# Integers in place of rounded floats: the feed-forward quantisations of a four-stage transformer kernel, one core

## The chip, the core and the metric

The kernel runs on one core of a Trainium2 chip. The metric is the device time of one launch in microseconds. The core has TensorE (PE, matrix products), VectorE (DVE), ScalarE (ACT), GpSimd (POOL) and SyncE (SP, which issues the transfers). Each has its own instruction stream; they meet only at semaphores.

## The reference, cut to what matters

`x` is 2x256 tokens of width 512. The reference adds four branches to it in turn: a quantised product with the context, a quantised gated feed-forward layer (`_L0_ffn_ref`), cross attention, and a mixture of experts. The change lies in the second:

```
def act_qdq(x, bits=16):
    qmax = 2 ** bits - 1
    mn = minimum(min(x), 0);  mx = maximum(max(x), 0)
    scale = maximum((mx - mn) / qmax, 1e-12)
    zp = clip(round(-mn / scale), 0, qmax)
    q = clip(round(x / scale) + zp, 0, qmax)
    return (q - zp) * scale
```

The layer projects up and gate (1376 wide) from the normalised tokens, quantises both with `act_qdq`, takes the sigmoid of the gate, rounds it to 16 bits with a fixed scale of 2^-16, multiplies sigmoid and gate, quantises that product, multiplies it by up, quantises again, and projects down. Each `act_qdq` needs the minimum and maximum over the whole tensor before its first element can be quantised. Weights are quantised to 4 bits in blocks of 32.

## The kernel before, in words

All tiles have 128 partitions and, mostly, 512 columns of float32. The feed-forward width 1376 makes FT = 11 tiles, so `up` and `gate` are 11 tiles of 128x512 each, with features on the partitions and tokens in the columns. Every stage is one hand-written order per engine, in loops over tiles; semaphores count finished tiles.

The stages in order of time: the *up* stretch (11 tiles), the *gate* stretch (11), the *down* stretch, in which the gate is quantised and passed through the sigmoid while the 11 down-projection weights are prepared and the value projection of the later attention (16 units of 12 matmuls, `v_unit`) runs on TensorE, the *product* stretch (sigmoid times gate, quantised, times up), the *output* stretch (quantise, split in a high and a low float16 half, 132 matmuls of the down projection). Between two stretches VectorE runs `parameters(k, ...)`: the extrema are reduced over columns, sent through two TensorE operations to reduce over partitions (`spread(k)` in TensorE's queue), and scale, zero point and bounds are put in `aqp[:, k]`.

A weight tile passes through all engines. VectorE takes block maxima (L1255), scales (L1225 on `dsc`) and a reciprocal (L1264); GpSimd divides (`divide`, L469); ScalarE rounds by adding and subtracting MAGIC (`round_weights`, two copies); GpSimd scales back (`scale_back`, L477); TensorE transposes (L999); ScalarE copies the high half out of PSUM (`weight_high`); VectorE takes the low half (`weight_low`, L1228 reading `ps`). Three tiles are under way at a time.

Rounding works the same way for activations: a float32 plus MAGIC = 12582912.0 has no fraction left. A quantisation is thus a ScalarE copy with scale and bias MAGIC (`quantise`), a clip on VectorE between `lo` and `hi`, and a subtraction of MAGIC, on VectorE with a multiplication (`dequantise`), or on ScalarE (`up_integer`):

```
def clip(dst, k):
    return ts(dst, dst, aqp[:, k, 1:2], ALU.max, aqp[:, k, 2:3], ALU.min)
```

In a down turn `i` VectorE clips gate tile i, clips the sigmoid of tile i-2, finishes gate tile i, multiplies tile i-2 (`gated`), takes one weight tile's maxima and low half, and the two extrema of the product (`extrema`, L1331 and L1332). ScalarE in the same turn quantises gate tile i+1, takes the sigmoid of tile i-1 (L722) and rounds it, copies the weight's high half, rounds the next weight, and copies a value tile out of PSUM twice (`v_out`). GpSimd has `v_low` (L492), the low half of a value tile.

The names `ts`, `tt`, `stt` and `copy` are helpers, so most VectorE operations stand at L1225 (TENSOR_SCALAR), L1222 (TENSOR_TENSOR) or L1228 (SCALAR_TENSOR_TENSOR), and ScalarE's at L583. All large tiles lie in one buffer, `arena`. `own.link` makes VectorE wait for its own last operation. In the queues, ScalarE's eight `attention_high` copies, which split the first attention weights together with GpSimd (`attention_split`: L518, L523), stand ahead of its part of the output stretch; their transfers start when all 16 value units are done.

## Time and profile before

| | us |
|---|---|
| median of 3 runs | 910.67 |
| lowest, highest | 909.2, 914.12 |
| profiled execution, device time | 910.75 |
| its span, first to last instruction | 908.9 |
| PE busy in it | 744.9 |
| DVE busy | 704.3 |
| ACT busy | 528.6 |
| POOL busy | 499.8 |

The mean granted TensorE clock is 0.921 of full speed. Busy times are shares of the whole span. What a single stage waits for has to be read from its own stretch: the down stretch lies at about 216 to 278 us, the product stretch at 282 to 316, the output stretch at 320 to 353, attention and experts behind 366.

### The profile page before, as it was taken

The page shows a single profiled execution, that of the slowest core. Times are in us where ns is not written, and L with a number is a line of the kernel's source. Part 1 is how long each engine was busy: PE and PEld are TensorE (multiplying, and loading weights), DVE is VectorE, ACT ScalarE, POOL GpSimd, SP SyncE. Part 2 cuts the span into 40 slices and gives each one's busy share as a digit, 9 for nine tenths or more (in the row PEclk, how much of TensorE's full clock was granted, in tenths as well). Part 3 has the DMA queues.
Part 4 walks back from the last instruction along what each step waited for, and adds up shares of the span by engine and source line. Part 5 has one row for each costly group of instructions (what it writes and reads, how often), then busy time and mean ns, then how long its engine had stood idle before and what let it go on. Part 6 is the DMA issues. An engine that isn't in the chain of part 4 may idle for free.

```text
span 908.9 us, 15108 instructions
## 1 busy us (share of the span) xinstructions
PE 744.9 (82%) x3482; PEld 352.1 (39%) x3483; DVE 704.3 (77%) x1432; ACT 528.6 (58%) x955; POOL 499.8 (55%) x472
## 2 busy tenths in 40 slices
PE   0379789677675076789999999999999768999997
PEld 0135444333232032334444444444444333444443
DVE  6976768788998973578888888888888656666666
ACT  3333457688774260467777777777776533455551
POOL 3953645653763700278878888888875321434341
PEclk9779979899888578989999999999999878999999
DMA  7210023121101003056666666666656620323321
GB/s 303 70 58 0 1 58 116 50 66 46 36 0 55 38 0 112 15 94 149 149 147 147 149 145 160 156 139 142 147 103 143 136 69 1 105 104 104 104 69 46
DMA packets 147599, 84.82 MB, mean 93 GB/s; under 512 B 137185, under 2 KB 137441, under 8 KB 144626
## 3 DMA queue, kind: packets, MB, share of 16 engines
q1 hardware_dynamic: 147570, 84.47, 36.0%
q8 instruction: 13, 0.21, 0.1%
q14 instruction: 16, 0.13, 0.0%
HBM read 49.85 MB, written 1.05 MB: 56 GB/s over the span
## 4 chain that ended last, share of the span: by engine, by line
PE 64%; DVE 19%; issue 6%; POOL 4%; ACT 3%; DMA 2%; DVEq 2%; POOLq 0%; ACTq 0%; SPq 0%
PE ps L908 20%; PE ps L909 20%; PE ps L910 19%; DVE arena L1228 5%; DVE arena L1225 4%; ACT arena L583 2%; DVE mm L1332 2%; PE ps L1102 1%; DVE arena L1222 1%; DVE mm L1331 1%; DVE dsc L1255 1%; PE ps L975 1%; POOL arena L477 1%; DVE dsc L1225 1%; POOL arena L542 1%
## 5 line engine op out<-in xcount | busy, mean ns | idle before, releaser
L908 PE MATMUL ps<-arena 128*128 128x512 f16 (+1 forms) x988 | 386.0, 391 | 32.5 <-POOL arena L401 11.4
L909 PE MATMUL ps<-arena 128*128 128x512 f16 (+1 forms) x988 | 386.1, 391 | 0.0
L910 PE MATMUL ps<-arena 128*128 128x512 f16 (+1 forms) x988 | 384.4, 389 | 0.0
L583 ACT ACTIVATE arena<-arena 128x512 f32 (+5 forms) x383 | 255.2, 690 | 135.4 <-DVE arena L1228 36.7
L1228 DVE SCALAR_TENSOR_TENSOR arena<-ps,arena 128x512 f32<-128x512 f32 (+2 forms) x186 | 125.7, 702 | 41.2 <-ACT arena L583 29.1
L908 PEld LDWEIGHTS ps<-arena 128*128 128x128 f16 (+1 forms) x988 | 99.0, 100 | 151.0 <-issue 29.4
L910 PEld LDWEIGHTS ps<-arena 128*128 128x128 f16 (+1 forms) x988 | 99.1, 100 | 124.0 <-issue 13.1
L909 PEld LDWEIGHTS ps<-arena 128*128 128x128 f16 (+1 forms) x988 | 98.8, 100 | 112.6 <-issue 10.3
L542 POOL TENSOR_SCALAR arena<-arena,rden 128x512 f32<-128x512 f32 x128 | 115.2, 900 | 30.6 <-DVE rden L1593 21.4
L1222 DVE TENSOR_TENSOR arena<-arena 128x512 f16<-128x512 f32 (+3 forms) x154 | 117.5, 795 | 7.2 <-ACT arena L583 6.4
L822 ACT ACTIVATE arena<-arena,mneg 128x512 f32<-128x512 f32 x128 | 91.4, 715 | 34.5 <-DVE mneg L1573 34.5
L583 ACT ACTIVATE arena<-ps 128x512 f16<-128x512 f32 (+4 forms) x114 | 64.4, 588 | 65.1 <-PE ps L949 39.4
L558 POOL TENSOR_TENSOR arena<-arena 128x1024 f16<-128x1024 f16 (+1 forms) x18 | 38.4, 2134 | 105.1 <-ACT arena L583 105.1
L1573 DVE CUSTOM_DVE_ANT_0 arena<-ps,arena 128x512 f32<-128x512 f32 x128 | 82.9, 686 | 3.4 <-issue 0.3
L523 POOL TENSOR_TENSOR arena<-arena 128x512 f32 (+1 forms) x64 | 74.6, 1187 | 0.2 <-ACT arena L583 0.2
L532 POOL TENSOR_TENSOR rk<-ss,nh 128x4 f32<-128x4 f32 x32 | 32.6, 1017 | 66.1 <-DVE ss L1225 66.1
L469 POOL TENSOR_TENSOR arena<-arena,dsi (+1 forms) x30 | 32.9, 1097 | 58.0 <-DVE dsi L1264 58.0
L518 POOL TENSOR_SCALAR arena<-arena 128x512 f32<-128x512 f32 x64 | 61.2, 970 | 3.7 <-DMA arena<-in_wq 1.4
L1228 DVE SCALAR_TENSOR_TENSOR arena<-ps,mbs,arena 128x512 f32<-128x512 f32 x36 | 27.0, 750 | 35.3 <-ACT arena L881 18.5
L583 ACT ACTIVATE arena<-ps,nws 128x512 f16<-128x512 f32 (+1 forms) x48 | 32.5, 677 | 33.1 <-PE ps L975 29.2
L999 PE MATMUL ps<-ident,arena 128*128 128x128 f32 x132 | 23.3, 304 | 33.3 <-POOL arena L477 16.9
L1228 DVE SCALAR_TENSOR_TENSOR arena<-arena 128x512 f16<-128x512 f32 (+2 forms) x40 | 37.0, 924 | 13.8 <-ACT arena L583 13.1
(114 smaller groups left out, 765.2 us busy)
## 6 DMA issues: line engine op xcount, KB each, us to landing
arena<-in_moe_w SPq DMA_DIRECT2D x18, 768.0 KB, 4.4
arena<-in_ffn_w SPq DMA_DIRECT2D x33, 256.0 KB, 2.7
arena<-in_wq SPq DMA_DIRECT2D x8, 1024.0 KB, 5.1
arena<-in_wo SPq DMA_DIRECT2D x8, 1024.0 KB, 5.2
arena<-in_kv_w SPq DMA_DIRECT2D x4, 1024.0 KB, 4.9
arena<-in_ctx SPq DMA_DIRECT2D x1, 2048.0 KB, 9.2
arena<-in_ctx_t SPq DMA_DIRECT2D x1, 2048.0 KB, 13.6
arena<-arena SPq DMA_TRANSPOSE x128, 3.3
```

The lines of the kernel that those rows point to most:

```text
L518: g.tensor_scalar(src, src, SW, 1.0, ALU.mult, ALU.mult).then_inc(aw_sc, 1)
L523: g.tensor_tensor(lo, src, hi, ALU.subtract).then_inc(aw_lo, 1)
L542: g.tensor_scalar(sc[:, h], sc[:, h], rden[:, h:h + 1], SP, ALU.mult, ALU.mult)\
L583: return a.activation(out_, in_, ACT.Copy, scale=scale, bias=bias)
L822: a.activation(sc[:, h], sc[:, h], ACT.Exp, bias=mneg[:, h:h + 1], scale=-1.0, accum_out=den[:, h:h + 1]).then_inc(a_e, 1)
L908: pe.matmul(out_, lhs[0], rhs[0], start=first, stop=False)
L909: pe.matmul(out_, lhs[0], rhs[1], start=False, stop=False)
L910: return pe.matmul(out_, lhs[1], rhs[0], start=False, stop=last)
L1222: return v.tensor_tensor(out_, x_, y_, op)
L1225: return v.tensor_scalar(out_, x_, s1, s2, o1, o2)
L1228: return v.scalar_tensor_tensor(out_, x_, s_, y_, o1, o2)
L1573: v.tensor_tensor_reduce(sc[:, h], bank(h), mk[:, t % 2], -1.0 / SXW, 3.0e38, ALU.add, ALU.min, mneg[:, h:h + 1]).then_inc(a_sm, 1)
```

## The change

Every activation quantisation of the feed-forward layer becomes one VectorE operation that multiplies by the inverse scale, takes the minimum with an upper bound, and writes int32, so that the write rounds. The zero point is dropped from the stored value, and the lower bound isn't applied. The tiles `upq` and `gateq` are the same bytes as `up` and `gate`, read as int32; `hi` in `aqp` becomes QMAX minus the zero point. ScalarE's `quantise`, `up_integer`, `out_quant` and the waits around them go. The sigmoid reads the integers with the scale as its operand, and a copy that writes uint16 (`s16`) rounds it. The product of sigmoid and gate, and the product with up, are `tensor_tensor_reduce`, which writes the product and its maximum over the columns; only the minimum (`least`) is left as an operation of its own. ScalarE's value copies no longer stand behind the parameters of the product stretch. VectorE's loops over the down, product and output stretches are written out in full.

```diff
+        upq, gateq = carve(150, (FT, TOK), I32), carve(172, (FT, TOK), I32)
+        s16 = carve(130, (2, TOK), U16)
...
             def gate_turn(n):
                 weight_high(n + 1)
-                if not isinstance(n, int) or n >= FT + 3:
-                    up_integer(n - FT - 3)
                 round_weights(n + 3)
                 tile_out(n, gate, sx4)
                 if isinstance(n, int) and n == FT:
                     kw_high(3)
-                    a.wait_ge(par_ready, 2)
-                quantise(up, 1, n - FT, u_y)
...
             def gate_sigmoid(i):
                 wait_apart(a, g_dq, i + 1, (in_ctt, 16))
-                a.activation(one(sig, i % 2), one(gate, i), ACT.Sigmoid).then_inc(own_a, 1)
+                a.activation(one(sig, i % 2), one(gateq, i), ACT.Sigmoid, scale=aqp[:, 2, 3:4]).then_inc(own_a, 1)
                 wait_apart(a, own_a, i + 1, (in_ctt, 16))
-                copy(one(sig, i % 2), one(sig, i % 2), 65536.0, MAGIC).then_inc(s_y, 1)
+                copy(one(s16, i % 2), one(sig, i % 2), 65536.0).then_inc(s_y, 1)
...
             def down_turn(i, more=True, rounds=True):
-                if more:
-                    gate_front(i + 1)
-                if not isinstance(i, int) or i >= 1:
-                    if not isinstance(i, int) or i >= 3:
-                        a.wait_ge(gs_done, i - 2)
-                    gate_sigmoid(i - 1)
+                if not isinstance(i, int) or i >= 2:
+                    a.wait_ge(gs_done, i - 1)
+                gate_sigmoid(i)
                 if more:
                     weight_high(2 * FT + i + 1)
...
-            a.wait_ge(par_ready, 4)
...
-            plain_loop(a, 0, 2 * MT - FT - 1, product_turn)
-            plain_loop(a, 2 * MT - FT - 1, FT, product_quant)
+            plain_loop(a, FT + 1, 2 * MT, v_out)
...
             def out_high(i):
                 a.wait_ge(o_int, i + 1)
-                copy(one(og[0], i), one(gate, i)).then_inc(o_hi, 1)
+                copy(one(og[0], i), one(gateq, i), SINT).then_inc(o_hi, 1)
...
+            def integer(dst, src, k):
+
+                return ts(dst, src, aqp[:, k, 0:1], ALU.mult, aqp[:, k, 2:3], ALU.min)
...
-                v.wait_ge(u_y, i + 1)
-                clip(one(up, i), 1).then_inc(u_cl, 1)
+                integer(one(upq, i), one(up, i), 1).then_inc(u_q, 1)
...
             def gate_front(i):
-                dequantise(gate, 2, i, g_y, g_dq)
+                integer(gateq[:, i], gate[:, i], 2).then_inc(g_dq, 1)
...
+            def gated(i):
                 v.wait_ge(s_y, i + 1)
+                v.tensor_tensor_reduce(gate[:, i], s16[:, i % 2], gateq[:, i], 1.0, -3.0e38, ALU.mult, ALU.max,
+                                       mm2[:, 0, i:i + 1]).then_inc(gs_done, 1)
...
+            def least(i, done):
+                v.wait_ge(done, i + 1)
+                own.mark(v.tensor_reduce(mm2[:, 1, i:i + 1], gate[:, i], AX.X, ALU.min, negate=True))
...
+            for i in range(2, FT):
+                gate_front(i)
+                gated(i - 2)
+                if i + 3 >= FT:
+                    weight_low(2 * FT + i)
+                    least(i - 2, gs_done)
+                else:
+                    weights(2 * FT + i, lambda: least(i - 2, gs_done))
...
+            def product_int(i):
+                integer(gateq[:, i], gate[:, i], 3).then_inc(p_int, 1)
+
+            def times_up(i):
+                v.wait_ge(p_int, i + 1)
+                v.wait_ge(u_q, i + 1)
+                v.tensor_tensor_reduce(gate[:, i], gateq[:, i], upq[:, i], 1.0, -3.0e38, ALU.mult, ALU.max,
+                                       mm2[:, 0, i:i + 1]).then_inc(p_done, 1)
...
             def out_int(i):
-                v.wait_ge(o_y, i + 1)
-                own.link(clip(one(gate, i), 4))
-                ts(one(gate, i), one(gate, i), MAGIC, ALU.subtract, SINT, ALU.mult).then_inc(o_int, 1)
+                integer(gateq[:, i], gate[:, i], 4).then_inc(o_int, 1)
```

Where the instructions stand now. On VectorE, one of the last turns of the down stretch (tile 8; `ps` is the weight's PSUM bank, `mm` the extrema), before:

```order
L1225 TENSOR_SCALAR arena<-arena,aqp 128x512 [waits g_y]
L1225 TENSOR_SCALAR arena<-arena 128x512 [waits s_y]
L1225 TENSOR_SCALAR arena<-arena,aqp 128x512 [waits own_v]
L1228 SCALAR_TENSOR_TENSOR arena<-arena 128x512 [waits own_v]
L1228 SCALAR_TENSOR_TENSOR arena<-ps,arena 128x512 [waits w_hi]
L1331 TENSOR_REDUCE mm<-arena 128x1 [waits gs_done]
L1332 TENSOR_REDUCE mm<-arena 128x1
```

and in the changed kernel, the same turn:

```order
L1183 TENSOR_SCALAR arena<-arena,aqp 128x512
L1416 ISA arena,mm<-arena 128x512 [waits s_y]
L1416 ISA mm 128x1
L1186 SCALAR_TENSOR_TENSOR arena<-ps,arena 128x512 [waits w_hi]
L1421 TENSOR_REDUCE mm<-arena 128x1 [waits gs_done]
```

Seven operations have become four and the short read of the accumulator (the second ISA row); the wait for ScalarE's quantise (`g_y`) is gone, the one for the sigmoid (`s_y`) has moved to the product itself.

On ScalarE, the opening of the down stretch, before:

```order
L583 ACTIVATE arena<-arena,aqp 128x512 [waits par_ready]
L583 ACTIVATE arena<-arena,aqp 128x512
L583 ACTIVATE arena<-ps 128x512 [waits f_ps,w_t]
L583 ACTIVATE arena<-arena 128x512 [waits w_div]
L583 ACTIVATE arena<-arena 128x512 [waits w_mag]
L583 ACTIVATE arena<-ps 128x512 [waits v_ps]
L583 ACTIVATE arena<-ps 128x512
L583 ACTIVATE arena<-arena,aqp 128x512
L722 ACT_TABLE_LOAD
L722 ACTIVATE arena<-arena 128x512 [waits g_dq]
```

and in the changed kernel:

```order
L709 ACT_TABLE_LOAD [waits g_dq]
L709 ACTIVATE arena<-arena,aqp 128x512 [waits par_ready]
L586 ACTIVATE arena<-arena 128x512 [waits own_a]
L586 ACTIVATE arena<-ps 128x512 [waits f_ps,w_t]
L586 ACTIVATE arena<-arena 128x512 [waits w_div]
L586 ACTIVATE arena<-arena 128x512 [waits w_mag]
L586 ACTIVATE arena<-ps 128x512 [waits v_ps]
L586 ACTIVATE arena<-ps 128x512
```

The table load and the first sigmoid with its rounding copy now stand ahead of the weight's high half (the row that waits for `f_ps,w_t`), and the three quantise copies are gone.

## Rows read from the trace of the kernel before

**Rows 1.** The head of the page.

```profile
span 908.9 us, 15108 instructions
```

**Rows 2.** Windows: stretch, its length, busy us (instructions) of PE, PEld, DVE, ACT, POOL, clock, DMA.

```profile
192.00:202.00 10.00, 7.99 (x41) 4.03 (x42) 9.36 (x18) 8.41 (x16) 4.10 (x4) 1.00 0.22 57
245.00:257.00 12.00, 7.74 (x33) 3.65 (x31) 12.00 (x21) 8.98 (x17) 8.00 (x6) 0.86 0.08 22
```

**Rows 3.** Timeline of VectorE, one down turn: start us, duration us, operation.

```profile
245.40 0.45 DVE L1225 TENSOR_SCALAR arena<-arena,aqp  x1
245.77 0.41 DVE L1225 TENSOR_SCALAR arena<-arena  x1
246.10 1.27 DVE L1225 TENSOR_SCALAR arena<-arena,aqp  x1
247.29 1.64 DVE L1228 SCALAR_TENSOR_TENSOR arena<-arena  x1
248.85 0.67 DVE L1255 TENSOR_REDUCE dsc<-arena  x1
249.45 0.67 DVE L1228 SCALAR_TENSOR_TENSOR arena<-ps,arena 128x512 f32 x1
250.04 0.16 DVE L1225 TENSOR_SCALAR dsc<-dsc  x1
...
251.47 0.45 DVE L1225 TENSOR_SCALAR arena<-arena,aqp  x1
```

**Rows 4.** Timeline of GpSimd, in the gate stretch and in the same down turn.

```profile
202.49 1.05 POOL L469 TENSOR_TENSOR arena<-arena,dsi  x1 [2.19 <-DVE dsi L1264]
...
245.84 1.25 POOL L469 TENSOR_TENSOR arena<-arena,dsi  x1 [2.07 <-DVE dsi L1264]
247.05 1.33 POOL L492 TENSOR_TENSOR arena<-arena  x1
```

**Rows 5.** Timeline of ScalarE, one down turn.

```profile
241.25 1.35 ACT L583 ACTIVATE arena<-arena  x2 [1.36 <-POOL arena L469]
...
243.49 0.72 ACT L583 ACTIVATE arena<-arena,aqp  x1
...
245.36 0.58 ACT L583 ACTIVATE arena<-ps 128x512 f32 x1
```

**Rows 6.** Timeline of ScalarE, opening of the down stretch.

```profile
215.50 1.33 ACT L583 ACTIVATE arena<-arena,aqp 128x512 f32<-128x512 f32 x2 [1.52 <-DVE aqp L1225]
...
220.10 1.28 ACT L722 ACT_TABLE_LOAD   x1
```

**Rows 7.** Timeline of VectorE: first and seventh product, ends of two stretches, parameters' end.

```profile
223.97 0.68 DVE L1228 SCALAR_TENSOR_TENSOR arena<-arena  x1
...
259.43 1.64 DVE L1228 SCALAR_TENSOR_TENSOR arena<-arena 128x512 f32<-128x512 f32 x1
...
278.42 0.17 DVE L1341 TENSOR_REDUCE ext<-mm 128x2 f32<-128x22 f32 x1
...
281.67 0.16 DVE L1222 TENSOR_TENSOR aqp<-aqp 128x1 f32<-128x1 f32 x1
...
316.52 0.17 DVE L1341 TENSOR_REDUCE ext<-mm 128x2 f32<-128x22 f32 x1
```

**Rows 8.** The one fused reduce (attention), by its line: count, then ns min/median/max.

```profile
L1573 DVE CUSTOM_DVE_ANT_0 arena<-ps,arena x128: 678/686/693, 378.8 to 720.7; 128x512 f32<-128x512 f32 x128
```

**Rows 9.** Timeline of TensorE: the last transposes and value units, start of the output stretch.

```profile
268.17 0.63 PE L999 MATMUL ps<-ident,arena 128*128 128x128 f32 x4 [1.13 <-DVE arena L1228]
...
276.18 0.38 PE L910 MATMUL ps<-arena 128*128 128x512 f16 x1
...
324.00 0.58 PE L908 MATMUL ps<-arena 128*128 128x512 f16 x1 [5.68 <-DVE arena L1222]
```

**Rows 10.** Timeline of GpSimd: first and last of the first attention weights' splits.

```profile
295.63 1.92 POOL L518 TENSOR_SCALAR arena<-arena 128x512 f32<-128x512 f32 x2 [1.38 <-DMA arena<-in_wq]
...
310.39 2.71 POOL L523 TENSOR_TENSOR arena<-arena 128x512 f16<-128x512 f32 x2
```

More of the change, by code:

```diff
@@ L7 @@
 BF16 = mybir.dt.bfloat16
+I32 = mybir.dt.int32
+U16 = mybir.dt.uint16
 ALU = mybir.AluOpType
@@ L683, in _ @@
             tile_out(FT - 1, up, sx4)
-            def quantise(src, j, i, done):
-                copy(one(src, i), one(src, i), aqp[:, j, 0:1], MAGIC).then_inc(done, 1)
-            def up_integer(i):
-                wait_apart(a, u_cl, i + 1, (in_ctt, 16))
-                copy(one(up, i), one(up, i), 1.0, -MAGIC).then_inc(u_int, 1)
             def gate_turn(n):
                 weight_high(n + 1)
-                if not isinstance(n, int) or n >= FT + 3:
-                    up_integer(n - FT - 3)
                 round_weights(n + 3)
@@ L774, in _ @@
                     attention_high(0, part, k)
[L775 to L778 removed]
             def out_high(i):
                 a.wait_ge(o_int, i + 1)
[L782 to L789 removed]
+                copy(one(og[0], i), one(gateq, i), SINT).then_inc(o_hi, 1)
+            plain_loop(a, 0, FT, out_high)
             hidden_high(1, SX)
@@ L1415, in weights @@
                 inverse_scales(n + 3, m)
-            def dequantise(dst, k, i, ready, done):
-                v.wait_ge(ready, i + 1)
-                own.link(clip(one(dst, i), k))
-                ts(one(dst, i), one(dst, i), MAGIC, ALU.subtract, aqp[:, k, 3:4], ALU.mult).then_inc(done, 1)
+            def integer(dst, src, k):
+                return ts(dst, src, aqp[:, k, 0:1], ALU.mult, aqp[:, k, 2:3], ALU.min)
             def with_tiles(base, after, per):
@@ L1447, in _ @@
             parameters(2, FT, 1.0)
+            own.link(ts(aqp[:, 2, 7:8], aqp[:, 2, 3:4], 2.0 ** -16, ALU.mult))
             def gate_front(i):
[L1451 to L1453 removed]
+                integer(gateq[:, i], gate[:, i], 2).then_inc(g_dq, 1)
+            def gated(i):
                 v.wait_ge(s_y, i + 1)
[L1455 to L1477 removed]
+                v.tensor_tensor_reduce(gate[:, i], s16[:, i % 2], gateq[:, i], 1.0, -3.0e38, ALU.mult, ALU.max,
[3 more added lines that the diff above has]
+                own.mark(v.tensor_reduce(mm2[:, 1, i:i + 1], gate[:, i], AX.X, ALU.min, negate=True))
             for i in range(2):
@@ L1481, in _ @@
             weights(2 * FT + 1)
-            own.loop(2, FT - 3, 6, down_turn)
-            for i in range(FT - 3, FT):
-                down_turn(i)
+            for i in range(2, FT):
[4 more added lines that the diff above has]
+                    least(i - 2, gs_done)
+                else:
+                    weights(2 * FT + i, lambda: least(i - 2, gs_done))
             for i in (FT - 2, FT - 1):
-                gated(i, sigmoid_clip(i))
-                gated_extrema(i)
+                gated(i)
+                least(i, gs_done)
             own.wait(own.n)
-            parameters(3, FT, 2.0 ** -16)
-            v.wait_ge(u_int, FT)
+            parameters(3, FT, aqp[:, 2, 7:8])
             own.link(tt(aqp[:, 3, 7:8], aqp[:, 3, 3:4], aqp[:, 1, 3:4], ALU.mult))
-            def product_clip(i):
-                v.wait_ge(p_y, i + 1)
-                clip(one(gate, i), 3).then_inc(p_cl, 1)
-            def times_up(i, more=True):
-                v.wait_ge(p_cl, i + 1)
-                stt(one(gate, i), one(gate, i), MAGIC, one(up, i), ALU.subtract, ALU.mult).then_inc(p_done, 1)
-                if more:
-                    product_clip(i + 1)
-                v.wait_ge(p_done, i + 1)
-                extrema(one(gate, i), i)
-            product_clip(0)
-            own.loop(0, FT - 1, 2, times_up)
-            times_up(FT - 1, False)
+            def product_int(i):
[5 more added lines that the diff above has]
+                                       mm2[:, 0, i:i + 1]).then_inc(p_done, 1)
+            product_int(0)
+            for i in range(FT):
+                times_up(i)
+                if i + 1 < FT:
+                    product_int(i + 1)
+                least(i, p_done)
             own.wait(own.n)
@@ L1512, in out_int @@
             def out_int(i):
-                v.wait_ge(o_y, i + 1)
-                own.link(clip(one(gate, i), 4))
-                ts(one(gate, i), one(gate, i), MAGIC, ALU.subtract, SINT, ALU.mult).then_inc(o_int, 1)
+                integer(gateq[:, i], gate[:, i], 4).then_inc(o_int, 1)
             def out_low(i):
                 v.wait_ge(o_hi, i + 1)
-                tt(one(og[1], i), one(gate, i), one(og[0], i), ALU.subtract).then_inc(o_lo, 1)
+                stt(og[1][:, i], gateq[:, i], SINT, og[0][:, i], ALU.mult, ALU.subtract).then_inc(o_lo, 1)
             out_int(0)
-            def out_turn(i):
-                out_int(i + 1)
+            for i in range(FT):
+                if i + 1 < FT:
+                    out_int(i + 1)
                 out_low(i)
-            own.loop(0, FT - 1, 1, out_turn)
-            out_low(FT - 1)
             for t in range(NT):
```

56 lines of the change are left out of this document (8 added, 48 removed).

## The prediction, made before the changed kernel ran

> **What bounds the kernel now.** I read the page first, then the busy time by stretches, then the timelines of the stages that the diff touches, engine by engine. The page gives a span of 908.9 us [rows 1]; the profiled execution took 910.75, so 1.85 us lie around the span, and it stands 0.08 us from the median of 910.67. The attention and expert stages from 366 us on are untouched by the diff, so only the feed-forward part counts: the gate stretch from 172 us, the down stretch (gate and sigmoid) from 216 to 278, the product stretch from 282 to 316, and the output stretch that starts TensorE again at 324.
>
> In the gate stretch VectorE is busy 9.36 of 10 us, in the down stretch 12.00 of 12, while TensorE has 7.74 of 12 [rows 2]. So VectorE sets the pace in the stages that change. One down turn repeats every 6.07 us, from the clip at 245.40 to the next at 251.47 [rows 3]. Its operations start one behind the other: clip 0.37, sigmoid clip 0.33, the gate's subtract and multiply 1.19, the product 1.56, block maxima 0.60, the low half of the weight 0.60, and the rest (two extrema, a small scaling, a reciprocal) 1.43.
>
> Two of these are long for a reason that GpSimd's rows show. The TENSOR_SCALAR at 246.10 ends at 247.37, just behind GpSimd's divide (245.84 to 247.09); the product at 247.29 ends at 248.93, 0.55 us behind the end of GpSimd's next operation (247.05 to 248.38) [rows 3, 4]. The same product takes 0.68 us where GpSimd is idle, at 223.97 [rows 7]. Reductions and the operation that reads PSUM keep 0.67 behind it [rows 3]. So on this trace a VectorE operation that goes SBUF to SBUF at the fast TENSOR_SCALAR rate, or that reads two SBUF tensors, waits for the GpSimd operation in flight, and the next GpSimd operation then waits for it.
>
> **The change, part by part.** *Gate stretch.* VectorE exchanges a clip for `integer`, one TENSOR_SCALAR of the same size; ScalarE loses a quantise and an `up_integer`. VectorE keeps its count and was busy 9.36 of 10 us, so this is hidden under it: 0, at best 2 us where the first turns waited for ScalarE. If VectorE's cover were gone, ScalarE's lost operations would be worth 11 times two of 0.72 [rows 5].
>
> *Start of the down stretch.* `gate_front` no longer waits for ScalarE's copy, but ScalarE now has the table load (1.28 us [rows 6]) and the first sigmoid ahead of the weight copy, for which VectorE's `weight_low` waits, and behind that the reciprocal, GpSimd's divide and TensorE's transposes. Parameters end near 215.4 (ScalarE starts on them at 215.50 [rows 6]); front 0.5, load 1.28, sigmoid and round 1.25, weight copy 0.5, low half and scales 1.0, the next front 0.4 and small waits of 0.2 put the first product at 220.5. It was at 223.97 [rows 7]: **3.5 us** gained.
>
> *Six full down turns.* Removed per turn on VectorE: the first clip (0.37), the sigmoid clip (0.33) and the separate maximum (0.60); the new front needs 0.37 and the fused product 0.61, the pitch that I take from the only fused reduce of this trace, 686 ns long like its neighbours [rows 8]. Uncovered, a turn needs 0.37+0.61+0.60+0.60+0.10+0.60+0.16 = 3.04. To it come waits for GpSimd, which has three operations a turn (divide, the low half of a value tile, scale back) of a little over 1 us each when unhindered (1.05 [rows 4]). Laying them side by side by the rule read above: the divide arrives 0.44 behind VectorE's front (245.84 against 245.40 [rows 3, 4]), so the product still goes first; the small scaling waits 0.9 for the second GpSimd operation, the next front 0.25 for the third: 4.2 us. In the turn after, GpSimd's divide was already waiting and goes ahead of the product: 5.0. They alternate, mean 4.6. ScalarE allows it: 241.25 to 245.86 was 4.6 without idle, less the quantise's 0.6 gives 4.0 [rows 5]. From the first product to the seventh it was 35.46 (223.97 to 259.43 [rows 7]); 6 times 4.6 is 27.6: **7.9 us**. The ends are 4.0 (ScalarE) and 5.1 (every exposed operation waits a whole one), that is 11.5 and 4.9.
>
> *Tail of the stretch.* From the seventh product to the end of the extrema it was 19.0 (259.43 to 278.42). VectorE's own work becomes about 10.5. Then TensorE is late next: one more block of transposes and matmuls (3.1), a wait for the low half of the last weight, then the transposes and three value units that took 8.2 us (268.17 to 276.4 [rows 9]), before the parameters' transpose, which stands behind them in its queue. I take 13.0: **6.0 us**, with ends at 11 and 15.
>
> *Product stretch.* From the end of the parameters at 281.67 to 316.52 it was 34.85 [rows 7], 11 turns of 3.15. Unhindered, a turn was 0.61+0.45+0.60+0.60 = 2.26, so GpSimd cost 0.9 a turn. The new turn is 0.61+0.45+0.60 = 1.66 unhindered and 2.55 beside GpSimd. GpSimd's weight splits begin at 295.63, 14.0 us behind the parameters, and last to 313.1 [rows 10]. They begin earlier now: the value copies no longer wait for the parameters, so the last two value units end about 3.5 us behind them, the transfer takes 5, and the splits start at 8.6 us. So about 4 turns run at 1.66 (two late GpSimd copies among them), 7 at 2.55: 0.75+6.6+17.9, about 26: **8.9 us**. Ends: 19.0 (no contention) and 28.9 (all turns at 2.55).
>
> *A wait that could take its place:* `out_high` stands behind the eight `attention_high` copies in ScalarE's queue, which wait for GpSimd's splits. The splits end 17.5 us after their start, at 26.1; the parameters end at 29.4. Covered, with 3 us to spare; if the product stretch came down to 19, the excess would be lost again.
>
> *Output stretch.* From 316.52 to TensorE's start at 324.00 it was 7.48 [rows 7, 9]. ScalarE's quantise (0.72) with its handover and VectorE's second TENSOR_SCALAR go: **1.6 us**. The 11 later tiles ran on VectorE faster than TensorE's 12 matmuls, and still do: 0. The dropped `lo` operation in two parameter blocks is 2 times 0.15: **0.3**.
>
> Sum: 3.5+7.9+6.0+8.9+1.6+0.3 = 28.2; 910.75 less 28.2 is 882.5, and less 0.1 for the median 882. The ends of all terms taken together give about 866 and 895.
>
> **The rivals.**
> 1. *The fused product runs at half rate.* In the trace the fused reduce has one PSUM source; here both are in SBUF, uint16 and int32. The plain two-source product ran at 0.68 from SBUF [rows 7], which speaks against it, but it writes no accumulator. Doubling 0.61 costs 22 times 0.61 = 13.4: 895. The Trainium skill, Vector Engine (DVE) Microarchitecture Reference, Points that are easy to get wrong, says that a scalar-tensor-tensor form with two SBUF sources that aren't bf16 halves its throughput, as no port is left for the accumulator; no run here shows it.
> 2. *GpSimd takes more of it back.* Down turns at 5.1 and all product turns at 2.55: 3.0+2.9 less, 888. For it: every exposed operation of the turn at 245 waited.
> 3. *More is gained.* Down turns near ScalarE's 4.0, product turns mostly unhindered, the gate stretch quicker at its start: 3.6+6+2 more, about 870. Against it: GpSimd's work is as long as before and now falls on fewer microseconds.
> 4. *Slower.* Integer streams cost several passes in `integer` and in the fused product, on the engine that sets the pace. There are 66 such operations on it (44 and 22). The gain of 28.2 is gone when they cost 0.43 us more each, in mean; at 0.6 more it is 39.6 lost, 922. Nothing in the trace reads or writes integers, so it can't be excluded; that other data types here (float16 results of 0.68) cost nothing extra speaks against.
> 5. *The pace doesn't follow VectorE,* since the weights' chain (divide, round, scale back, transposes) holds 6.07 anyway: only product and output remain, 897 to 900. Against it: GpSimd and ScalarE wait in each turn, VectorE never [rows 2].
>
> **How the numbers follow.** Forecast 0.50, with its own range 876 to 889; rival 1 0.15; rival 2 0.14; rival 3 0.13; rival 4 0.03; rival 5 0.05. The range 866 to 895 takes in the first three rivals and leaves out about 0.1, more if rival 1 lies past its price. Half a per cent (4.6 us) is what this kernel's timing can tell: faster 0.95, same 0.02, slower 0.03.
>
> **What would show it.** Down turns of 4.2 to 5.0 us in place of 6.07; the fused product at 0.69 us where GpSimd is idle; the first down product 5.1 us behind the parameters; TensorE's parameter transpose directly behind its value units; the product stretch at about 26 us with GpSimd's splits 8.6 us into it; TensorE starting again some 6 us behind the last extremum. It is wrong if the fused product is well above 0.7 us alone, if `integer` loses the fast rate (from 0.54 to about 0.7: 44 times 0.15 is 6.6), if TensorE's clock falls below the 0.86 of the old down stretch and its turns of then 6 us set the pace, or if the output stretch waits for `attention_high`.

## The result and the profile after

The changed kernel takes 886.55 us (median of 4 runs, 884.26 to 888.29) against 911.28 for the kernel before in the same sitting: a ratio of 0.973, 95% interval 0.971 to 0.976. Its profiled execution took 888.29 us. The forecast was 882, its range 866 to 895.

The page's head, and the windows of the two stretches of [rows 2] and of the product stretch (columns as there):

```profile
span 886.5 us, 14686 instructions
```

```profile
188.00:198.00 10.00, 8.93 (x46) 4.33 (x45) 9.12 (x18) 6.27 (x11) 5.67 (x6) 1.00 0.25 74
230.00:242.00 12.00, 9.75 (x46) 4.12 (x44) 10.45 (x22) 10.89 (x20) 9.72 (x9) 1.00 0.15 44
261.00:289.00 28.00, 4.01 (x19) 1.63 (x17) 27.80 (x47) 7.11 (x12) 20.10 (x19) 0.66 0.21 76
```

In the down stretch VectorE was busy 12.00 of 12 us [rows 2]; now VectorE has 10.45, ScalarE 10.89, GpSimd 9.72, and TensorE runs at 1.00 in place of 0.86. No engine is full there any more. In the product stretch VectorE is still full, but part of that is waiting for GpSimd, which the profile shows as busy time.

VectorE's timeline, for the places of [rows 3, 7]: a short and a long down product, the last product of the stretch, then the ends of the two stretches.

```profile
225.67 0.68 DVE L1416 CUSTOM_DVE_ANT_0 arena<-arena 128x512 f32<-128x512 uint16 x1
...
229.07 0.59 DVE L1183 TENSOR_SCALAR arena<-arena,aqp 128x512 int32<-128x512 f32 x1
229.58 1.53 DVE L1416 CUSTOM_DVE_ANT_0 arena<-arena 128x512 f32<-128x512 uint16 x1
231.05 0.08 DVE L1416 DVE_READ_ACCUMULATOR2_ANT mm<- 128x1 f32 x1
231.05 0.67 DVE L1213 TENSOR_REDUCE dsc<-arena 128x16 f32<-128x512 f32 x1
232.10 0.69 DVE L1186 SCALAR_TENSOR_TENSOR arena<-ps,arena 128x512 f16<-128x512 f32 x1 [0.38 <-ACT arena L586]
...
255.75 1.59 DVE L1416 CUSTOM_DVE_ANT_0 arena<-arena 128x512 f32<-128x512 uint16 x1
...
258.11 0.17 DVE L1299 TENSOR_REDUCE ext<-mm 128x2 f32<-128x22 f32 x1
...
289.31 0.17 DVE L1299 TENSOR_REDUCE ext<-mm 128x2 f32<-128x22 f32 x1
```

GpSimd, beside the long product:

```profile
229.51 1.05 POOL L472 TENSOR_TENSOR arena<-arena,dsi  x1
```

The product that starts at 229.58 lasts until 231.11, 0.55 us behind the end of this divide. The fused product shows as CUSTOM_DVE_ANT_0 with a read of its accumulator of 0.08 us that lies under the next operation. Its two lines as groups (count, then ns shortest/median/longest, first and last start):

```profile
L1416 DVE CUSTOM_DVE_ANT_0 arena<-arena x11: 677/1533/1647, 216.4 to 255.8; 128x512 f32<-128x512 uint16 x11
```

```profile
L1449 DVE CUSTOM_DVE_ANT_0 arena<-arena x11: 674/1040/1656, 262.2 to 287.9; 128x512 f32<-128x512 int32 x11
```

Read by stretches, from one mark to the next. The marks are the extrema behind the up, gate, down and product stretches, the first and seventh down product, and the first addition of the output (352.80 before, 324.51 after):

| stretch, us | before | after | gained | predicted |
|---|---|---|---|---|
| up to the extrema behind up | 159.94 | 159.65 | 0.3 | 0 |
| gate stretch | 52.32 | 48.35 | 4.0 | 0 |
| to the first down product | 11.71 | 8.41 | 3.3 | 3.5 |
| six down turns | 35.46 | 26.49 | 9.0 | 7.9 |
| tail | 18.99 | 15.21 | 3.8 | 6.0 |
| to the extrema of the product | 38.10 | 31.20 | 6.9 | 8.9 |
| to the first output addition | 36.28 | 35.20 | 1.1 | 1.6 |
| to the end of the span | 556.1 | 562.0 | -5.9 | 0 |

With 0.3 predicted for the parameters, which lie within these stretches, 28.2 were predicted up to the output's first addition and 28.3 were gained, in partly different places; and 5.9 are given back in attention and experts, whose code is the same.

### The profile page after: what moved, and what is told of

The parts are those of the page before. It is cut to its first block, busy times and chain, and to the rows that moved or that the text cites. A ratio compares the mean times of both kernels' runs of the same rounds, so it can differ in the third digit from the quotient of the medians.

```text
span 886.5 us, 14686 instructions
## 1 busy us (share of the span) xinstructions
PE 742.7 (84%) x3483; PEld 350.9 (40%) x3483; DVE 674.3 (76%) x1396; ACT 497.0 (56%) x900; POOL 496.8 (56%) x472
## 3 DMA queue, kind: packets, MB, share of 16 engines
HBM read 49.85 MB, written 1.05 MB: 57 GB/s over the span
## 4 chain that ended last, share of the span: by engine, by line
PE 65%; DVE 17%; issue 5%; ACT 4%; POOL 4%; DMA 3%; DVEq 1%; ACTq 1%; SPq 1%; POOLq 0%
PE ps L866 20%; PE ps L867 20%; PE ps L868 20%; ACT arena L586 3%; DVE arena L1186 3%; DVE arena L1183 3%; DVE arena L1180 1%; PE ps L1060 1%; DMA arena<-arena 1%; DVE arena L1449 1%; DVE dsc L1183 1%; DVE mm L1421 1%; POOL arena L545 1%; DMA arena<-in_moe_w 1%; POOL arena L472 1%
## 5 line engine op out<-in xcount | busy, mean ns | idle before, releaser
L586 ACT ACTIVATE arena<-arena 128x512 f32 (+7 forms) x372 | 248.5, 691 | 147.5 <-DVE arena L1186 36.8
L1180 DVE TENSOR_TENSOR arena<-arena 128x512 f16<-128x512 f32 (+2 forms) x143 | 109.9, 803 | 7.6 <-ACT arena L586 7.2
L1186 DVE SCALAR_TENSOR_TENSOR arena<-ps,nws,arena 128x512 f16<-128x512 f32 (+1 forms) x48 | 35.8, 746 | 9.2 <-ACT arena L586 8.4
L1180 DVE TENSOR_TENSOR arena<-ps,rk 128x512 f32<-128x512 f32 (+1 forms) x48 | 33.0, 687 | 9.4 <-PE ps L933 7.5
```

The lines of the kernel that those rows point to most:

```text
L586: return a.activation(out_, in_, ACT.Copy, scale=scale, bias=bias)
L1180: return v.tensor_tensor(out_, x_, y_, op)
L1186: return v.scalar_tensor_tensor(out_, x_, s_, y_, o1, o2)
```

## The experiments

Twelve kernels, each timed in 4 to 6 runs. The first is the changed kernel itself and the last combines four edits; the others are the changed kernel with one edit. Two numbers are steadier than the time and are used beside it: the length of a stretch, which repeats within 0.1 us in most of these profiles, and the part behind the first output addition ("the rest").

### The changed kernel again

> The changed kernel once more, with nothing edited. It gives a second profile beside the one of 888.29 us. Theory A: the 5.9 us that the attention and expert stages gave back (the first output add stood 28.3 us earlier, the end 22.4) come from where TensorE's granted clock happens to step between its two levels, which the program does not set; then the time from the first output add at 324.51 to the end of the span at 886.5 (562.0 us) differs here by 2 us or more, and the stretches before it repeat within 0.5 us. Theory B: the loss belongs to the new alignment of the program; then the 562.0 repeats within 1 us. Time about 886.5 either way.

886.36 us, ratio 0.972. Tail, down turns and product stretch repeat within 0.03 us (26.47, 15.21, 31.23), the gate stretch is 49.57 in place of 48.35, the first output addition comes at 324.40, the rest is 562.4. So a loss of about 6 us behind the output isn't an accident of one execution: theory B by its number. But its parts don't repeat. One accumulator read of ScalarE in attention (at 470.36 before the change) stands 117.56 us behind the first output addition before it, 120.96 in the first profile of the changed kernel and 123.21 in this one. So 3.4 and 5.7 us are lost up to there, and 2.5 and 0.7 behind it; that the sums agree within 0.5 us is in part chance. The kernel before has one profile only. The gate stretch has two lengths, 48.3 to 48.4 in nine profiles and 49.3 to 49.6 in three, with this kernel in both groups.

### What the fusion is worth

```diff
-                v.tensor_tensor_reduce(gate[:, i], gateq[:, i], upq[:, i], 1.0, -3.0e38, ALU.mult, ALU.max,
-                                       mm2[:, 0, i:i + 1]).then_inc(p_done, 1)
+                tt(gate[:, i], gateq[:, i], upq[:, i], ALU.mult).then_inc(p_done, 1)
...
+                own.mark(v.tensor_reduce(mm2[:, 0, i:i + 1], gate[:, i], AX.X, ALU.max))
```

> Only the fusion of the product with up is undone: TENSOR_TENSOR and a separate maximum in each of the 11 turns of the product stretch, integers and everything else as in the changed kernel. Theory A: VectorE's own time plus what GpSimd adds sets a turn, so each maximum costs its 0.60: 11 times 0.60 = 6.6, the stretch from the end of the parameters 27.9 -> 34.5, time about 893. Theory B: beside GpSimd the turn is paced by GpSimd's operations and the maximum falls in time that VectorE would wait; then only the 4 or 5 undisturbed turns pay, about 2.7, stretch 30.6, time about 889. Theory C: the fused form costs as much as its two parts: no difference.

The stretch is 35.14, 3.9 more than 31.20: between A and B. Eleven maxima are 6.6 us of work, of which 2.7 fall into time that VectorE spent waiting for GpSimd. The time is 887.76, only 1.4 above the kernel of the experiment before, and the intervals of the two ratios overlap: the fusion's worth is seen in the stretch and not in the time. In the two profiles the rest was 3.2 and the gate stretch 1.3 shorter here, which hides the 3.9.

The same edit on the down product (`s16` times `gateq`):

> Only the fusion of sigmoid and gate is undone: TENSOR_TENSOR and a separate maximum, 11 times in the down stretch. The product stretch taught that a maximum of 0.60 is partly hidden beside GpSimd: 3.9 of 6.6 us were paid there. Theory A: VectorE, its own work and its waits for GpSimd, sets the down turn of 4.42: turns of 4.8 to 5.0, from the first to the seventh product 26.5 -> 29.4, and 1 to 2 more in the tail, time about 891. Theory B: ScalarE sets the turn and VectorE has slack for the maximum: 26.5 stays within 0.5, time within 1 us of 886.5.

From the first to the seventh product 28.91 in place of 26.49: 0.40 a turn. Neither theory: VectorE has slack for a third of the maximum. The time of 887.25 doesn't tell it from the changed kernel either.

### Which engine sets the down turn

```diff
                 gate_sigmoid(i)
+                copy(spare[:, 0], xres[:, 0])
```

> One more ScalarE copy of a 128x512 float32 tile into a spare tile in each of the 11 down turns, behind the sigmoid's rounding; it takes 0.6 to 0.7 us and nobody waits for its result. Theory A: VectorE and GpSimd set the turn of 4.42 and ScalarE has room: the six turns stay near 26.5 us, time 886.5. Theory B: ScalarE is the engine that sets it since the change: turns of 5.0 to 5.1, 26.5 -> about 30.3, and 1 to 2 in the tail, time about 891. Both this and the undone fusion slow: then neither engine alone sets the pace, but a ring of waits between the two.

28.79, 0.38 a turn, and now an even 4.8 from one product to the next, with ScalarE busy 9.45 of 10 us in it. With the experiment before, both slow, so the third case that was written down holds: no single engine sets the 4.42. ScalarE's work is about 4.0 of it (busy 10.89 of 12 us), as the prediction had it; the rest is waits, where VectorE's low half stands for ScalarE's copy (0.38 at 232.10 above) and ScalarE's rounding for GpSimd's divide. The tail was 1.3 shorter in this profile and the product stretch 1.9 longer. Time 888.49.

### The gate stretch

Two copies of a constant tile are put where `up_integer` and `quantise` stood, and the wait for the parameters with them.

> ScalarE gets its two operations of a gate turn back, at their old places and with the old wait for the parameters, but as copies of a constant 128x512 float32 tile into spare tiles, so that VectorE doesn't wait for them. Everything else as in the changed kernel, whose gate stretch, from the extrema behind the up stretch to those behind the gate stretch, is 48.35 us (159.65 to 208.00), 4.0 shorter than before. Theory A: ScalarE's load is what was shortened: the stretch goes back to about 52.3, time 890.5. Theory B: the gain comes from VectorE, whose old clip stood behind ScalarE's rounding, and ScalarE has room for 1.4 us more in a turn of 4.4: the stretch stays within 0.5 of 48.35, time 886.5. Theory C: both, 50 to 51.

48.77: theory B. ScalarE was busy 26.0 us of 30 in this stretch with its operations back, 24.8 before the change and 19.0 after it, and the length hardly follows. Time 886.17.

What differs is on VectorE. In the kernel before, the small scaling and the step into the loop body, one gate turn of 4.24 us:

```profile
186.62 0.98 DVE L1225 TENSOR_SCALAR dsc<-dsc  x1
...
190.25 0.69 DVE L1228 SCALAR_TENSOR_TENSOR arena<-ps,arena 128x512 f32 x1 [0.32 <-issue]
190.86 0.97 DVE L1225 TENSOR_SCALAR dsc<-dsc  x1
```

GpSimd beside the first of them:

```profile
186.51 1.05 POOL L477 TENSOR_TENSOR arena<-arena,dsc 128x512 f32 x1
```

and after, two turns that take 7.5 together:

```profile
184.38 0.67 DVE L1186 SCALAR_TENSOR_TENSOR arena<-ps,arena 128x512 f32 x1
184.97 0.38 DVE L1183 TENSOR_SCALAR dsc<-dsc  x1
...
188.29 0.69 DVE L1186 SCALAR_TENSOR_TENSOR arena<-ps,arena 128x512 f32 x1 [0.59 <-ACT arena L586]
188.90 0.70 DVE L1183 TENSOR_SCALAR dsc<-dsc  x1
...
191.86 0.67 DVE L1186 SCALAR_TENSOR_TENSOR arena<-ps,arena 128x512 f32 x1
```

The scaling of 128x16 elements takes 0.17 us alone; 0.98 is a wait for GpSimd's operation of 1.05 in flight, shown as busy time. It shrank to 0.38 and 0.70, and the 0.32 of issue went; a wait of 0.59 for ScalarE stands in every second turn in its place. Which of the edits shifted the two engines against each other (the clip that no longer waits for `u_y`, or the loop body without that wait) wasn't tried separately.

### The table load

```diff
             v_out(0)
+            a.activation(spare[:, :], nws[:, 0:1], ACT.Sigmoid)
             a.wait_ge(par_ready, 3)
```

> One sigmoid of one column on a spare tile is added in ScalarE's queue ahead of the wait for the gate's parameters, so that the table load of 1.28 us falls into that wait. Theory A: the load stands on the path to the first down product (sigmoid, rounding, product): it comes about 1.3 us earlier, 8.4 -> 7.1 us behind the extrema, time about 885.2. Theory B: the weight chain (ScalarE's high half, VectorE's low half) or the first gate tiles set the start, and nothing is gained: 886.5.

The first down product comes 7.13 us behind the extrema in place of 8.41: 1.28 gained, exactly the load's length in the profile; theory A. The time is 882.89, 3.5 less than the changed kernel in the same sitting, of which the load explains 1.3: in this profile the product stretch was 30.60 and the rest 558.0. The Trainium skill, ScalarE: Activation LUTs, What ACT_TABLE_LOAD costs, adds a drain to the load and gives 2.66 us for a switch; the stretch gained 1.28, so the drain cost nothing on this path.

### GpSimd beside the product stretch

```diff
             sp.wait_ge(v_ps, 2 * MT)
+            sp.wait_ge(p_done, FT - 2)
...
+            for i in range(FT):
+                out_high(i)
+                if 1 <= i <= 6:
+                    attention_high(0, (i + 1) // 4, (i + 1) % 4)
```

> The first attention weights are loaded when nine products with up are done, in place of when the 16 value units are done, and ScalarE takes two attention_high copies ahead of the output stretch and the other six behind out_high 1 to 6. So GpSimd is idle in most of the product stretch. Theory A (VectorE's SBUF operations wait for GpSimd's): the stretch goes from 27.9 to about 20.5 (10 turns of 1.67, the first ones beside the two last value copies, some 2 us), 7.4 gained, and the output stretch, where TensorE takes 2.6 us a tile against VectorE's 1.06, keeps its length: time about 879. Theory B (the long operations have another cause, such as int32 or uint16 operands): stretch 27.9, time 886.5. Theory C: the wait comes back in the output stretch, because VectorE's first integer copies now meet GpSimd's splits: 3 to 5 us given back, about 883.

Extrema to extrema 23.85 in place of 31.20: 7.35 gained, theory A to 0.1 us. The window of the stretch, and then two turns of VectorE in it:

```profile
260.00:281.00 21.00, 3.83 (x19) 1.56 (x17) 20.68 (x47) 2.17 (x4) 2.91 (x3) 0.65 0.16 55
```

```profile
274.26 0.67 DVE L1452 CUSTOM_DVE_ANT_0 arena<-arena 128x512 f32<-128x512 int32 x1
274.86 0.53 DVE L1186 TENSOR_SCALAR arena<-arena,aqp 128x512 int32<-128x512 f32 x1
...
275.92 0.67 DVE L1452 CUSTOM_DVE_ANT_0 arena<-arena 128x512 f32<-128x512 int32 x1
```

The same 47 operations of VectorE, with GpSimd busy 2.91 us beside them in place of 20.10, take 20.68 in place of 27.80. All eleven fused products last 0.67 to 0.69. Some of theory C came too: TensorE starts 6.92 us behind the extrema, not 5.75, since two small operations of the parameters and the first integer copies now met the splits; but the first addition comes 35.00 behind the extrema, 0.2 earlier than without the edit. Time 879.24, ratio 0.964 [0.962, 0.967].

The Trainium skill, SBUF — State Buffer, Who interferes with whom, says that VectorE and GpSimd lock each other out for a whole instruction when VectorE's runs in a two-port mode, or has two SBUF inputs while GpSimd's reads SBUF, and that reductions never contend. The rows agree: the reductions of the product stretch stay at 0.67 to 0.69 in the changed kernel and in this one.

The edit also moves the transfers of the attention weights and ScalarE's copies of them. That these made the long operations is ruled out in the changed kernel itself, in a stretch in which the transfers run and ScalarE and GpSimd are idle:

```profile
268.20:269.80 1.60, 0.00 (x0) 0.00 (x0) 1.60 (x5) 0.00 (x0) 0.00 (x0) 1.00 1.04 435
```

The fused product at 268.88 takes 0.67 us there and the integer copy at 269.49 0.53. The product at 225.67 takes 0.68 beside a busy ScalarE.

### The earlier value copies

```diff
+            a.wait_ge(par_ready, 4)
             plain_loop(a, FT + 1, 2 * MT, v_out)
```

> ScalarE's last value copies (12 to 15) wait again for the parameters of the product stretch, as in the kernel before. Theory A: only the order of GpSimd's work changes: its four value operations leave the tail (15.2 us, perhaps 0.5 to 1 shorter) and fall behind the parameters, the splits start 14 us behind them in place of 8.4 and end 31 us behind them, just as the next parameters are ready: the product stretch of 27.9 stays within 1, time 886 to 888. Theory B: the splits end too late, and ScalarE's first out_high waits for its attention_high copies: the output stretch starts 1 to 4 us later, time 888 to 890.

The extrema of the product come 29.67 us behind those of the down stretch, 1.5 earlier than in the changed kernel, and TensorE starts 6.25 behind them, 0.5 later, as GpSimd ends 3.8 us behind the extrema. Neither theory had this as it came: theory A had the stretch within 1 us and the tail shorter, and theory B's late start is only 0.5. The tail stays at 15.21: the first of these copies reached GpSimd at 257.86, behind the last product. Time 886.06. Moving the value copies, one of the edits, bought nothing: it moved the splits from 13.5 to 8.4 us behind the parameters, and so the end of them, which could lie behind the stretch, back into it.

### What makes the tail

> The changed kernel, but GpSimd's low halves of the value tiles 9 to 15 are taken of one column in place of 512; the rest of these halves is set to zero beforehand, in GpSimd's idle time at 209 to 216 us. So the values lose that part of their precision; every wait is kept. In the changed kernel these copies stand beside VectorE's last three down products (1.65, 1.40, 1.59 us long) and the first product turns. Theory A: GpSimd makes the tail 15.2 us long; the extrema come up to 2.5 us earlier (12.7 to 13.5 behind the seventh product), but TensorE, which worked without a gap until 258.45, is late next: the parameters' transpose stays 15.5 us behind the seventh product, the parameters come no earlier, and only the product stretch gains, 1 to 2 us. Time 884.5 to 886. Theory B: GpSimd's copies cost nothing in the tail, because ScalarE's sigmoids set its turns: 15.2 again. Theory C: TensorE isn't late either and the parameters come 2 us earlier: time about 883.

VectorE at the end of the stretch, and TensorE's transpose of the extrema:

```profile
251.96 0.68 DVE L1425 CUSTOM_DVE_ANT_0 arena<-arena 128x512 f32<-128x512 uint16 x1
...
254.24 0.68 DVE L1425 CUSTOM_DVE_ANT_0 arena<-arena 128x512 f32<-128x512 uint16 x1
...
255.56 0.68 DVE L1425 CUSTOM_DVE_ANT_0 arena<-arena 128x512 f32<-128x512 uint16 x1
...
257.01 0.18 DVE L1308 TENSOR_REDUCE ext<-mm 128x2 f32<-128x22 f32 x1
259.79 0.28 DVE L1310 TENSOR_REDUCE row<-ps 2x1 f32<-2x128 f32 x1 [2.60 <-PE ps L908]
```

```profile
259.48 0.27 PE L908 MATMUL ps<-ident,ext 128*2 128x128 f32 x1
```

The extrema come 13.1 us behind the seventh product (243.93), 2.1 earlier, and VectorE then waits 2.60 for TensorE, whose transpose stands 15.55 behind that product as before: theory A. Two engines end the tail together: VectorE beside GpSimd, and TensorE's value units. The product stretch, from the first integer copy to the extrema, is 24.2 in place of 27.7, more than the 1 to 2 expected. The rest was 562.1; time 885.56, ratio 0.969 in its sitting.

That the time lies in theory A's range is luck, because the edit has a cost that its text put at nothing. The memset in GpSimd's idle time held up the gate's parameters. VectorE's row, then GpSimd's:

```profile
206.92 3.18 DVE L1192 TENSOR_SCALAR row<-ident,row 2x2 f32<-2x2 f32 x1
```

```profile
207.00 3.08 POOL L504 MEMSET arena<- 128x3584 f16 x1
```

The same 2x2 operation takes 0.22 us in the changed kernel. The first down product comes 11.38 us behind the extrema in place of 8.41, so 3.0 us of what the shorter copies win is lost at the start.

### TensorE's clock

```diff
+            def warm(n):
+                for _ in range(n):
+                    pe.matmul(bank(6), kt[0][:, 0, 0:P], kt[0][:, 0, 0:D], start=True, stop=True)
...
+            warm(30)
             hidden_transposes(1)
...
             q_unit(0, 0)
+            warm(12)
```

> The changed kernel with 42 matmuls more that nobody reads: 30 behind the down projection, where TensorE was idle for 8.3 us, and 12 behind the first query unit, where it was idle for 3.5 us. From the first output add to the end it was 556.1 us before the change and 562.0, 562.4, 559.3, 561.7, 558.0, 558.6, 562.0, 559.8 and 560.8 in the profiles of the changed kernel and its variants. Theory A: the 2 to 6 us lost there are TensorE at 1.2 GHz behind its own idle gaps, and how the gaps fall against the steps of the clock decides: with the gaps filled the first 80 us of it run at 2.4 GHz and the rest is at or below 558, time about 883. Theory B: the clock falls for another reason (a transfer, the other engines): 558 to 562 as before, time 886.5. The second gap, at the start of the experts, is left as it was, so 1.7 us may stay.

Here are two places on TensorE in three kernels: the transposes of the hidden tiles, and the first query transposes with what follows. Before the change:

```profile
362.99 3.28 PE L949 MATMUL ps<-ident,arena 128*128 128x128 f32 x16 [8.29 <-DVE arena L1225]
...
374.08 0.66 PE L1102 MATMUL ps<-ident,arena 128*128 128x128 f32 x4 [3.49 <-DVE arena L1222]
374.57 0.38 PE L908 MATMUL ps<-arena 128*128 128x512 f16 x1
374.79 0.38 PE L909 MATMUL ps<-arena 128*128 128x512 f16 x1
```

After it:

```profile
334.71 3.60 PE L907 MATMUL ps<-ident,arena 128*128 128x128 f32 x16 [8.30 <-DVE arena L1183]
...
345.98 1.11 PE L1060 MATMUL ps<-ident,arena 128*128 128x128 f32 x4 [3.49 <-DVE arena L1180]
346.89 0.63 PE L866 MATMUL ps<-arena 128*128 128x512 f16 x1
347.31 0.63 PE L867 MATMUL ps<-arena 128*128 128x512 f16 x1
```

With the gaps filled:

```profile
324.78 6.64 PE L898 MATMUL ps<-arena 128*128 128x512 f16 x30
333.24 1.97 PE L911 MATMUL ps<-ident,arena 128*128 128x128 f32 x16 [1.82 <-DVE arena L1189]
...
339.71 2.75 PE L898 MATMUL ps<-arena 128*128 128x512 f16 x12
343.36 0.66 PE L1065 MATMUL ps<-ident,arena 128*128 128x128 f32 x4 [0.90 <-DVE arena L1186]
343.86 0.38 PE L866 MATMUL ps<-arena 128*128 128x512 f16 x1
```

The idle times ahead of both places are the same before and after the change (8.3 and 3.49 us), yet before it the matmuls behind the second have a pitch of 0.216 us, 2.4 GHz, and after it 0.43, 1.2 GHz. The first block is slow in both (3.28 and 3.60); only before the change was the clock up again by the second. With the gaps filled the two blocks take 1.97 and 0.66, and the rest is 555.7, the 556.1 of the kernel before. The windows behind the second place give the granted clock (the third number from the end), before and after the change:

```profile
373.80:380.00 6.20, 5.83 (x28) 2.74 (x28) 2.95 (x7) 3.05 (x4) 1.01 (x1) 1.00 0.00 0
```

```profile
345.00:351.70 6.70, 5.72 (x16) 2.63 (x17) 1.44 (x2) 0.69 (x1) 0.20 (x1) 0.50 0.00 0
```

Theory A; time 882.15, ratio 0.967 [0.964, 0.970]. At ScalarE's accumulator read in attention, the mark used above, the eleven profiles of kernels with these two gaps unfilled lie 3.2 to 5.8 us behind the kernel before, and this one 0.6. Behind the mark the differences go from 2.2 us gained to 2.5 lost, in code that no edit touches; no run explains these.

The other gap, ahead of the output stretch, is filled by 14 and 8 such matmuls on either side of the parameters' last matmuls:

> The changed kernel with 22 matmuls more on TensorE that nobody reads, 14 when eight products with up are done and 8 behind the parameters' second operation, so that TensorE works in the 36 us in which it was idle ahead of the output stretch. In the changed kernel the output matmuls start at 295.06 with a pitch of 0.43 us and change to 0.216 at 300.14. Theory A: the granted clock follows what TensorE itself did just before; the output stretch starts at 0.216, the first output add comes 35.2 - 2.5 = 32.7 us behind the extrema, time about 884. Theory B: the extra matmuls stand in the way of the parameters or the clock stays low: 35 or more, 886.5 to 888. The later attention may still give some of it back.

TensorE's timeline:

```profile
293.36 3.30 PE L898 MATMUL ps<-arena 128*128 128x512 f16 x8
297.37 0.38 PE L866 MATMUL ps<-arena 128*128 128x512 f16 x1 [0.72 <-DVE arena L1192]
297.59 0.38 PE L867 MATMUL ps<-arena 128*128 128x512 f16 x1
```

The output matmuls start at 0.216, and the first addition comes 32.40 us behind the extrema in place of 35.20. Theory A. The rest was 558.5, so that more than the 2.8 us of the output shows in the time: 882.24, ratio 0.967 [0.963, 0.970].

### All together

> The late splits, the early table load, the 22 matmuls ahead of the output stretch (now from seven products on) and the 42 around the start of attention in one kernel. The stretches add up if they are independent: from 879.2 (late splits alone), 1.3 for the table load, 2.5 for the output stretch and 3 at the start of attention: about 872.5. If the clock gives back what the stretches win, 876 to 879.

873.62 us (871.29 to 875.95), ratio 0.958 [0.955, 0.961] to the kernel before: faster than both kernels. Product stretch 23.86, start 7.13, rest 554.1. Only the output stretch gained nothing (34.93): its first integer copies meet the splits, TensorE idles 2.15 us ahead of it and starts at 1.2 GHz again.

## Why the prediction was right, and where its terms were not

The mechanism was right where VectorE sets the pace: operations that leave it shorten the stretch, and GpSimd takes part of it back. In the down stretch it holds only until ScalarE's and GpSimd's work come near VectorE's; then no engine alone sets the turn. Part of the agreement of the sum is luck, as the terms show:

- *Gate stretch, 0 predicted, 4.0 measured.* The step that failed is "VectorE keeps its count and was busy 9.36 of 10 us, so this is hidden under it". Over the 30 us from 172 on it was busy only 25.7, and 0.8 of a turn's 4.24 was a wait for GpSimd that the profile shows as busy time of a small operation, as the same text had read such waits in the down stretch. The experiment shows that ScalarE's relief isn't the reason; that VectorE and GpSimd meet less is seen in the rows, which edit did it is open.
- *Start, 3.5 and 3.3.* Right. The table load stood on this path at its 1.28, as the moved load shows.
- *Down turns, 7.9 and 9.0.* 4.42 a turn, not 4.6. The turns last 4.63, 4.63, 3.91, 4.63, 4.78 and 3.91: short where the product goes ahead of GpSimd's divide and the low half waits little for ScalarE, long where either fails, so not in strict alternation. The prediction priced no wait for ScalarE here; the rows have such waits of up to 0.85. The added operations show a slack of some 0.1 to 0.2 us a turn on VectorE and on ScalarE.
- *Tail, 6.0 and 3.8.* The mis-sized term is the 13.0, on both of its sides. "VectorE's own work becomes about 10.5": beside GpSimd's operations the last five products took 1.40 to 1.65 us each, not 0.6. "TensorE is late next" was right, but it is later than 13.0: with the value copies cut short the extrema come at 13.1, and TensorE's transpose still stands 15.55 us behind the seventh product.
- *Product stretch, 8.9 and 6.9.* The prediction's own summands, 0.75+6.6+17.9, give 25.25 and not the 26 that it took; measured were 27.9. The splits started 8.4 us in (8.6 predicted). The four turns ahead of them took 8.3 us, not 6.6, because two of them meet GpSimd's late value copies (integer copies of 1.37 and 1.36), which were named and not priced. Behind them six turns take 2.89 each, mean between 270.54 and 287.87, in place of 2.55, since in some turns more than one operation waits, and the last is undisturbed: 18.8 for the seven, not 17.9. With the splits moved away the term was 14.3 (38.10 to 23.85).
- *Output, 1.6 and 1.7* at TensorE's start (5.75 in place of 7.48); 0.6 of it is lost again before the first addition: from TensorE's start to there it is 29.45 us in place of 28.80.
- *Attention and experts, 0 and -5.9.* The step that failed is "untouched by the diff, so only the feed-forward part counts". At attention's start, where 3.4 of the 5.9 are lost, the cause is TensorE at 1.2 GHz behind its idle gaps: filling them brought it back. Why the same gaps cost less before the change isn't shown; that the later stages came at another time against the steps of the clock is the likely reason. The other 2.5 us, most of them around the start of the experts, weren't tested, and this part varies from profile to profile.
- *The ends.* "The ends of all terms taken together give about 866 and 895" doesn't come out of the terms: added up, they give about 868, with the gate's 2 us, and 890. The 895 is the price of rival 1.

Rival 1 is refuted: where GpSimd is idle, the fused product takes 0.67 to 0.69 us with uint16 or int32 beside a second SBUF operand, and it takes 1.0 to 1.66 only beside GpSimd. The rule of the Trainium skill (Vector Engine (DVE) Microarchitecture Reference, Points that are easy to get wrong) doesn't show on this form. Rival 4 too: the integer write keeps the fast rate, 0.45 to 0.55 us, as the clips of floats before it. Rival 2 was nearly right for the product stretch (28.9, measured 27.9) and wrong for the down turns. Rival 3 named the gate stretch rightly and the product turns wrongly. Rival 5 falls with the turn of 4.42. The forecast of the sum held because two terms that were too high (tail, product, 4.2 together) met two that were too low (gate, down turns, 5.1); that the time lies 4.5 us above 882 comes from the rest.

## What to carry to other kernels

When VectorE bounds a stretch, subtract from its busy time what its operations last longer than the same ones do alone: that part belongs to GpSimd, and moving GpSimd's transfers and splits to a stretch where TensorE is the bound was worth more here (7.35 us) than either fusion. The same holds for an experiment: a memset put in GpSimd's idle time cost 3.0 us through an operation of 2x2 elements. A gain ahead of an untouched stage can be lost in it when the stage begins with idle gaps on TensorE; here 42 cheap matmuls in those gaps brought it back. Fuse a reduction into a product when VectorE is full and little else waits, and expect less than its length (0.36 and 0.40 of 0.60 here) when another engine is near its limit.

## What the runs showed of the hardware

- A multiply and minimum that writes int32 (128x512) takes 0.45 to 0.55 us where GpSimd is idle, and up to 1.46 beside it.
- The fused multiply and maximum costs 0.67 to 0.69 us for 128x512 where GpSimd is idle, the same as the plain product; its accumulator read of 0.08 lies under the next operation.
- With equal idle times in front of it, the same transpose block ran at 2.4 GHz in one program and at 1.2 in another; what decides it is not shown by a run. In eleven profiles of kernels with the unfilled gap the rest lay between 558.0 and 562.4.
- A GpSimd memset of 128x3584 float16 takes 3.08 us, and a VectorE operation of 2x2 elements beside it 3.18 in place of 0.22.
